# Two expert stages: 71 row tiles instead of 72, the first rows fetched at the end of the stage before, and another order for the first eight tiles

## The reference

```python
x = x + 0.5 * ffn(layernorm(x))        # expert stage 1
x = x + attention(layernorm(x))        # 16 heads of 8, causal
x = x + 0.5 * ffn(layernorm(x))        # expert stage 2
# ffn: each token belongs to one of 8 experts (the largest affinity), and is kept if its
# rank among the batch's tokens for that expert is under a capacity; a kept token gives
#   gelu(x @ W1[e] + b1[e]) @ W2[e] + b2[e]        (128 -> 512 -> 128)
# a token that is not kept goes through as zeros, which leaves a constant row of the biases
```

## Time and profile before

| | |
|---|---|
| timed runs (3) | 1042.62, 1045.26, 1045.6 us; median 1045.26 |
| profiled execution | 1035.15 us, its span 1033.3 us |
| PE busy | 896.4 us (87%) |
| DVE, ACT, POOL busy | 724.8, 607.5, 682.8 us |

### The profile page before, as it was taken

The page is one execution under the profiler, slowest core; times in us unless marked ns, Lnnn a source line. Parts: engine busy times, 40 slices in busy tenths (PEclk is TensorE's granted clock), DMA queues, the critical chain, the costliest instruction groups (busy, mean ns, idle before and its releaser), DMA issues. The chain is left out here.

```text
span 1033.3 us, 26499 instructions
## 1 busy us (share of the span) xinstructions
PE 896.4 (87%) x8219; PEld 679.6 (66%) x8219; DVE 724.8 (70%) x2368; ACT 607.5 (59%) x1581; POOL 682.8 (66%) x1247
## 2 busy tenths in 40 slices
PE   5937499999647999999999999999999873999995
PEld 5823399999623566565656666565656542999995
DVE  8879745444237889899998989998898845444441
ACT  2637366666313666676666666666666651766662
POOL 7709668643023678888888888888887773355554
PEclk9999799999958999999999999999999985999998
DMA  7450022223145544446354554545454102222220
GB/s 214 128 173 1 17 69 67 69 66 64 40 79 106 122 96 101 115 94 122 95 116 101 109 108 97 121 95 117 95 115 97 39 24 61 60 67 67 64 59 21
DMA packets 127407, 89.72 MB, mean 87 GB/s; under 512 B 14305, under 2 KB 117910, under 8 KB 127270
## 3 DMA queue, kind: packets, MB, share of 16 engines
q1 hardware_dynamic: 103078, 52.69, 22.8%
q10 hardware_dynamic: 15488, 17.74, 7.7%
q0 software_dynamic: 8704, 17.60, 6.6%
HBM read 52.23 MB, written 35.47 MB: 85 GB/s over the span
## 5 line engine op out<-in xcount | busy, mean ns | idle before, releaser
L1291 ACT ACTIVATE at_pt<-at_pm 128x512 f32<-128x512 f32 x384 | 228.5, 598 | 117.9 <-PE at_pm L1379 84.2
L1609 DVE TENSOR_REDUCE at_mx<-at_pp 128x2 f32<-128x512 f32 (+1 forms) x384 | 259.5, 678 | 44.7 <-PE at_pp L1368 37.1
L1207 POOL TENSOR_SCALAR_AFFINE_SELECT at_pt<-at_pt 128x256 f32<-128x256 f32 (+1 forms) x384 | 187.8, 493 | 57.4 <-ACT at_pt L1291 54.1
L925 ACT ACTIVATE e_ht<-e_ps_h,b1t 128x128 f32<-128x128 f32 x576 | 164.8, 370 | 98.2 <-PE e_ps_h L954 98.2
L964 PE MATMUL e_ps_y<-w,e_ht 128*128 x1152 | 159.2, 282 | 0.0
L954 PE MATMUL e_ps_h<-e_xnt,e_w1own 128*128 128x128 f32 x1152 | 154.8, 279 | 1.4 <-issue 1.4
L954 PEld LDWEIGHTS e_ps_h<-e_xnt,e_w1own 128*128 128x128 f32 x1152 | 143.0, 195 | 1.6 <-issue 1.6
L964 PEld LDWEIGHTS e_ps_y<-w,e_ht 128*128 128x128 f32 x1152 | 140.0, 192 | 1.7
L1011 DVE SCALAR_TENSOR_TENSOR e_y<-e_ps_y,e_x 128x256 f32<-128x256 f32 x72 | 30.6, 425 | 155.7 <-PE e_ps_y L964 155.7
L888 POOL DMA_INDIRECT out_dram<-e_y,e_x x72 | 73.6, 1022 | 86.4 <-DVE e_y L1011 74.8
L1400 PE MATMUL at_po<-at_pt,vp 128*32 128x256 f32 (+1 forms) x2048 | 109.8, 332 | 1.6 <-POOL at_pt L1207 1.6
(11 more groups left out here) (327 smaller groups left out, 1788.6 us busy)
## 6 DMA issues: line engine op xcount, KB each, us to landing
at_qkd<-at_part SPq DMA_DIRECT2D x64, 192.0 KB, 3.0
kb<-at_qkd SPq DMA_DIRECT2D x64, 96.0 KB
qs<-at_qkd ACTq DMA_DIRECT2D x64, 96.0 KB
e_x<-buckets SPq DMA_DIRECT2D x72, 66.0 KB, 1.9
x<-e_y SPq DMA_DIRECT2D x36, 128.0 KB, 1.8
rows<-ts_x ACTq DMA_DIRECT2D x16, 264.0 KB, 3.0
ts_x<-in_x_dram SPq DMA_DIRECT2D x16, 256.0 KB, 3.5
x_by_token<-at_xa SPq DMA_DIRECT2D x32, 128.0 KB
```

The costliest lines, as they stand in the source:

```text
L925: last = a.activation(hid_t[j % NB][:, f, :], ps_h[j % NB][:, f, :], ACT.Gelu, bias=c.b1t[:, ds(e, 1), f])
L1207: g.affine_select(out=tile, in_=tile, compare_op=ALU.is_ge, fill=0.0, base=0, pattern=[[0, n], [1, P]], channel_multiplier=-1).then_inc(ma ...
L1291: a.activation(pt[u % RING][:, :], pm[u % 2], ACT.Exp, scale=SCALE).then_inc(exped, 1)
L1609: v.tensor_reduce(out, src, axis=AX.X, op=ALU.max).then_inc(maxed, 1)
```

## The change

- `NTE = NT + E - 1 = 71` takes the place of `NS = 72` in `experts`: 36 pairs still, the last of one tile. The buffer `x1` in HBM is a tile shorter.
- `x_row` and its semaphores are made once, in `consts`, and live through all stages. So that they fit, `at_p` in `route` no longer has a buffer of its own but uses the buffers of `c.qs`, which attention fills later.
- At the end of `route`, POOL waits for `gidx` and issues the gathers of the first 16 tiles of e1. At the end of `attention`, SP waits for `base`, reads 16 row numbers, waits as before for the buckets, and issues the loads of the first 16 tiles of e2. DVE converts `base` before `eid` there. The stages themselves start with tile 16 (`HEAD_PAIRS = 8`).
- In `experts` the start is written out: on PE `turn_x(0)`, `expand(0)`, `expand(1)`, `turn_x(1)`, `contract(0)`, `expand(2)`, and so on, the register loads of the expert numbers come first on PE and after the first copy on ACT, and the wait for the constant rows and W2 stands before the first `contract`. On DVE two W1 copies stand before the first `keep`, the others between the normalisations.

The core of the diff:

```diff
+NTE = NT + E - 1
+NR, HEAD_PAIRS = 8, 8
@@ consts
+    c.x_row = [m.sb(f"e_x{k}", [P, 2, XW]) for k in range(NR)]
+    c.x_in = {tag: [m.sem(f"{tag}_xin{k}") for k in range(NR)] for tag in ("e1", "e2")}
@@ route
-        at_p = sb("atp", [P, NT, P], BF16)
+        at_p = [q[:, :, :].rearrange("p h s -> p (h s)").rearrange("p (n w) -> p n w", w=P) for q in c.qs]
@@ route, POOL
+            pool.wait_ge(gidx_done, 1)
+            for j in range(2 * HEAD_PAIRS):
+                pool.indirect_dma_start(c.x_row[j // 2][:, j % 2, :], None, io["rows"],
+                                        bass.IndirectOffsetOnAxis(ap=c.gidx[:, j:j + 1], axis=0)).then_inc(c.x_in["e1"][j // 2], 16)
@@ route, DVE
-            s.step(v.tensor_copy(c.gidx[:, 0:NS], gsrc[:, :]))
+            v.tensor_copy(c.gidx[:, 0:NS], gsrc[:, :]).then_inc(gidx_done, 1)
@@ experts
-        NU = NS // 2
+        NU = -(-NTE // 2)
@@ experts, POOL
-                for j in range(2 * NR):
-                    gather(j)
-                for j in range(NS - 2 * NR):
+                for j in range(NTE - 2 * HEAD_PAIRS):
@@ experts, SP
-                for j in range(NS):
+                for j in range(2 * HEAD_PAIRS, NTE):
@@ experts, ACT
+            turn_x(0)
+            e = experts_of(act, 0)
+            bend(0, e[0])
+            turn_x(1)
+            bend(1, e[1])
+            bend(2, e[2])
+            turn_x(2)
+            bend(3, e[3])
+            turn_x(3)
+            bend(4, e[4])
+            for i in range(1, NU):
@@ experts, PE, in contract
+                if j == 0:
+                    pe.wait_ge(c.cst_in, 16 * 3)
+                    pe.wait_ge(c.w2_in, 16)
@@ experts, PE
-            pe.wait_ge(c.cst_in, 16 * 3)
-            pe.wait_ge(c.w2_in, 16)
-            for i in range(-TURN, NU):
-                if i + TURN < NU:
+            e = experts_of(pe, 0)
+            turn_x(0)
+            expand(0)
+            expand(1)
+            turn_x(1)
+            contract(0, e[0])
+            expand(2)
+            turn_x(2)
+            contract(1, e[1])
+            expand(3)
+            turn_x(3)
+            expand(4)
+            for i in range(1, NU):
+                if TURN < i + TURN < NU and i > 2:
                     turn_x(i + TURN)
...
+                    if i <= 2 and j == 2 * i:
+                        turn_x(i + TURN)
@@ experts, DVE
-            for j in range(FETCH):
-                fetch(j, e[j])
-            for i in range(-NORM, NU):
+            fetch(0, e[0])
+            fetch(1, e[1])
+            for i in range(NORM):
+                keep(i)
+                norm(2 * i)
+                norm(2 * i + 1)
+                if i == 0:
+                    fetch(2, e[2])
+                    fetch(3, e[3])
+                if i == 2:
+                    fetch(4, e[4])
+            for i in range(NU):
+                if i == 0:
+                    fetch(5, e[5])
@@ attention, SP
-            sp.wait_ge(tailed, 16 * E)
-            for k in range(NQ):
-                sp.wait_ge(row_out[k], 32 * (B // NQ))
+            sp.wait_ge(based, 1)
+            for j in range(0, 2 * HEAD_PAIRS, 8):
+                _, r = nc.values_load_multi_w_load_instructions(
+                    c.base[0:1, j:j + 8], engines=[sp.engine], min_val=0, max_val=E * STRIDE,
...
+                if j == 0:
+                    sp.wait_ge(tailed, 16 * E)
+                    for k in range(NQ):
+                        sp.wait_ge(row_out[k], 32 * (B // NQ))
+                for i in range(j, j + 8):
+                    sp.dma_start(c.x_row[i // 2][:, i % 2, :], io["buckets"][ds(r[i - j], P), :]).then_inc(c.x_in["e2"][i // 2], 16)
```

More of the change, by code:

```diff
@@ L544, in route @@
         zeroed = sem("zeroed")
-        far_done, near_done = sem("far"), sem("near")
+        far_done, near_done, gidx_done = sem("far"), sem("near"), sem("gidx")
         NA = 2
@@ L599, in _ @@
                     act.wait_ge(iota_done, 1)
-                of = slice((g + 1) * TG - NA, (g + 1) * TG)
+                first = (g + 1) * TG - NA
+                of = at_p[first // PN][:, first % PN:first % PN + NA, :]
                 for n in range((g + 1) * TG - NA, (g + 1) * TG):
-                    last = a.activation(at_p[:, n, :], iotab[:, :], ACT.Abs, scale=-1.0, bias=colp[:, n:n + 1])
+                    last = a.activation(at_p[n // PN][:, n % PN, :], iotab[:, :], ACT.Abs, scale=-1.0, bias=colp[:, n:n + 1])
                 last.then_inc(far_done, 1)
                 act.wait_ge(far_done, g + 1)
-                a.activation(at_p[:, of, :], at_p[:, of, :], ACT.Relu, scale=-1.0, bias=1.0).then_inc(near_done, 1)
+                a.activation(of, of, ACT.Relu, scale=-1.0, bias=1.0).then_inc(near_done, 1)
                 act.wait_ge(s_done, g + 1)
@@ L643, in invert @@
                 for n in range(g * TG, (g + 1) * TG):
-                    last = te.matmul(ps_inv, at_p[:, n, :], at_t[:, :, n, :],
+                    last = te.matmul(ps_inv, at_p[n // PN][:, n % PN, :], at_t[:, :, n, :],
                                      start=(n == 0), stop=(n == NT - 1), skip_group_check=True)
@@ L805, in sem @@
             return t.sem(f"{tag}_{name}")
[L807 removed]
+        NU = -(-NTE // 2)
         OUTS = 16 if by_slot else 32
[L809 removed]
+        NN, NX, NB = 8, 3, 4
         NORM, TURN, FETCH, BEND = 4, 3, 4, 3
         IDS = 8
[L812 removed]
+        x_row, x_in = c.x_row, c.x_in[tag]
         y_row = [t.sb(f"{tag}_y{k}", [P, 2, D]) for k in range(NR)]
@@ L882, in _ @@
             else:
-                for j in range(NS):
+                for j in range(NTE):
                     s = (j // 2) % NR
@@ L909, in _ @@
             for k in range(NR):
-                sp.wait_ge(y_out[k], OUTS * len(range(k, NU, NR)))
+                sp.wait_ge(y_out[k], sum(16 if by_slot else 16 * tiles_of(i) for i in range(k, NU, NR)))
         @blk.scalar
@@ L944, in turn_x @@
                 wait(pe, x_tr_out, i - 1)
-                for j in (2 * i, 2 * i + 1):
+                for j in range(2 * i, upto(i)):
                     pe.wait_ge(xn_done, j + 1)
@@ L1185, in _ @@
             blank_tails(sp, 0)
-            sp.wait_ge(tailed, 16 * E)
-            for k in range(NQ):
-                sp.wait_ge(row_out[k], 32 * (B // NQ))
+            sp.wait_ge(based, 1)
+            for j in range(0, 2 * HEAD_PAIRS, 8):
+                _, r = nc.values_load_multi_w_load_instructions(
+                    c.base[0:1, j:j + 8], engines=[sp.engine], min_val=0, max_val=E * STRIDE,
+                    skip_runtime_bounds_check_because="a tile's first row is at most that of the blank rows behind the last bucket, E * STRIDE")
+                if j == 0:
[4 more added lines that the diff above has]
+                    sp.dma_start(c.x_row[i // 2][:, i % 2, :], io["buckets"][ds(r[i - j], P), :]).then_inc(c.x_in["e2"][i // 2], 16)
         @blk.gpsimd
```

67 lines of the change are left out of this document (36 added, 31 removed).

## The result

The changed kernel takes 1058.76 us (median of 4 runs, 1057.13 to 1059.99), the kernel before 1044.46 beside it: a ratio of 1.0137, 95% interval 1.0122 to 1.0153. That is +14.3 us, slower as forecast, and just over half of the +26.0 that was forecast.

A forecast was written before the change was run, and what follows sets the result against it. PE was taken to bound the running expert stages, with all engines meeting at stage ends. Terms of +18.3 us in e1 and +7.7 in e2 gave +26.0 on 1045.26: 1071 us forecast, range 1061 to 1077.

The forecast's parts named there:

- The moved gathers hold POOL and the meeting point: End of route: 16 gathers take 20.15 us beside nothing; with POOL's drain the meeting point moves +25.8 us.
- Rival C: Ends of route and attention: the issue doesn't hold the meeting points, only gains stand, -10.3 us, 1035; chance 0.06.
- Rival D: Route: gathers cost POOL only the instruction's 0.95 us each, 4.8 us less, +21, 1066; chance 0.06.
- I take 6.2: End of route: POOL's drain behind the moved gathers takes 6.2 us, as in e1; 3.3 was the lower end.
- rival A: End of route: the drain is short or overlaps, its six microseconds aren't paid, +19.8, 1065; chance 0.10.
- rival B: The drain grows with the burst to twice 6.2, or SP stalls again: +33.9, 1079; chance 0.06.
- e1's start, -5.5: From DVE's first e1 instruction, first finish at 12.2 us and third at 22.2 instead of 27.7: -5.5 us.
- 71 tiles: One tile less: -2.0 us of PE work in e1, -1.6 us in e2's tail of scatters on POOL.
- SP's loads, +10.5 less 1.2: 16 loads add 10.5 us at the end of attention; e2's start gets 1.2 us shorter.
- the long instruction: Among e2's loads on SP, one DMA instruction of 1.99 us instead of 0.33, counted in the 10.5 us.
- The term for 8.8: End of attention: SP's 16 loads cost 8.8 us if the one long DMA instruction is absent.
- The timed runs' median is 10.1 us above that execution and I add the same: Whole kernel: the profiled execution of 1035.15 us lies 10.1 us under the timed median; same offset added after the change.

The follow-up runs named there:

- after_again: The changed kernel run once more against the kernel before, on a chip of the 1034-us level: 1054.35 us, ratio 1.0190.
- before_third: The kernel before, unchanged, under a second name and traced, at the 1034-us level: ratio 1.0005 to the kernel before.
- after_third: The changed kernel run a third time against the kernel before, on a chip of the 1045-us level: 1059.80 us, ratio 1.0129.
- before_fourth: The kernel before, unchanged, under a second name and traced, at the 1045-us level: ratio 1.0006 to the kernel before.
- g0l0: The changed kernel with gathers and loads both back in their own stages, leaving 71 tiles and the new order: 1028.47 us, ratio 0.9934 to the kernel before.
- late_loads: The changed kernel with the 16 loads back in e2 and the gathers still in route: 1048.06 us, ratio 1.0133 to the kernel before.
- g0: The changed kernel with all 16 gathers back in e1 and the loads still in attention: 1036.01 us, ratio 1.0021 to the kernel before.
- the pause: The kernel before with 22 us of POOL memsets ahead of the end of route: 1055.84 us at the lower level, 1066.85 at the upper.
- old71: The kernel before with only the 71 tiles, nothing moved and the old order: 1042.31 us, ratio 0.9963 to the kernel before.
- g8: The changed kernel with 8 gathers in route, the other 8 in e1, loads kept in attention: 1052.97 us, ratio 1.0078 to the kernel before.

## Why the prediction was right in its direction and wrong in its size

The stages as the traces have them, in us: the forecast, the change at the 1034-us level (after_again less before_third) and at the 1045-us level (after_third less before_fourth, from two chips of that level).

| from ... to | forecast | 1034 | 1045 |
|---|---|---|---|
| start to S | +25.8 | +22.1 | +22.2 |
| S to third finish | -5.5 | -5.7 | -12.6 |
| third to last finish of e1 | -2.0 | -1.8 | -1.8 |
| last finish to `base` | 0 | -1.5 | +1.0 |
| `base` to third finish of e2 | +9.3 | +6.3 | +7.1 |
| from there to the end | -1.6 | -1.5 | +0.8 |
| sum | +26.0 | +17.9 | +16.7 |
| timed | | +20.3 | +14.4 |

(Single executions of the kernel before lie between 1029.5 and 1038.6 at the lower level, and its three traces there differ by up to 1.9 us in `attention` alone; the two chips of the upper level differ by 1.9 us in its median. So a column meets its timed difference only to about 3 us.)

- **The moved gathers hold POOL and the meeting point: right.** 20.0 us for 16 (forecast 20.15), with all other engines idle. Rival C is out. Rival D is out as well: the gaps of 0.30 us stayed. The Trainium skill says in "DMA: Bandwidth & Descriptors" (Issuing engines are not separate DMA queues) that the time to initiate a DMA is usually small relative to the DMA itself. The traces don't agree for these gathers: 1.25 us each on POOL, against 2.6 from issue to landing (median, before_third).
- **"I take 6.2" for the drain behind them: wrong.** It took 2.3; this is rival A's side, which I gave 0.10, and rival B, a drain that grows with the burst, is out. I had both ends, 3.3 and 6.2, and chose by likeness of the DMAs instead of by how many the stage had issued. 3.9 us too much, of which 0.7 came back since `gidx` was written that much later.
- **e1's start, -5.5: right in its working** (12.2 and 22.2 us against 12.0 and 22.0), from a trace without the stop. Only 2.6 us of it are the moved gathers' (g0l0 against after_again).
- **71 tiles: right in e1** (-1.8). In e2 -1.5 at the lower level. At the upper one the tail isn't to be read, since the pairs' pace differs between its two chips (4.11 and 4.07 us).
- **SP's loads, +10.5 less 1.2: too much.** 8.7 of busy time without the long instruction, 6.3 to 7.5 net by traces, late_loads and g0. The term for 8.8 was in the text, and I carried the long instruction over as if it were part of the loads. It isn't: all eight traces of the kernel before, with the pause or without, have one of 1.22 to 1.99 us among e2's first 16 loads, and no kernel of 71 tiles has one over 0.72, not even where the loads stay in e2 (old71: 0.54). So it belongs to the start of e2 in the kernel before; what makes it is not shown.
- **"The timed runs' median is 10.1 us above that execution and I add the same": the step that failed most.** The 10.1 us are not an offset that stands beside every kernel. before_fourth less before_third, 10.3 us of span, says where they are: 0.8 to S, 6.75 in e1's stop, 0.6 to the next pair, 1.3 in `attention`, and 1.9 in e2's pairs (4.07 against 4.01 us), less 0.4 before e2's first finish and 0.6 behind its last. The profiled execution of 1035.15 us has the lower level's first finish and e2 pair (139.12 and 4.01), the kernel after's the upper level's pair (4.11), and the timed runs of both the upper level's times. That the kernel before was profiled on one chip and timed on another is my reading of these; no row says it. The change removes its gathers from just where those 7 us lie. Worked over with what the later traces measured, the forecast is 26.0 - 3.9 + 0.7 - 3.0 (loads and e2's start, 9.3 against 6.3) - 6.9 (S to third finish, -12.6 against -5.7) = +12.9, beside +14.3 measured.

What would have shown it: a median 1% above the profiled execution, in a range of 3 us that doesn't reach down to it, was a sign that the trace and the times are of two conditions. And the timeline of the kernel before, with a first finish at 139.1, already held a small stop in front of the same tile, which I passed over:

```profile
136.95 1.13 PE L954 MATMUL e_ps_h<-e_xnt,e_w1own 128*128 128x128 f32 x8 [1.43 <-issue]
```

What makes the three engines wait in the stop is left open. The gathers beside it are necessary (after_third, g8), and so is something in which the chips differ. An instruction stream that comes late to PE's queue would look like PE's gaps, but it would not explain ACT and DVE, which wait for products that PE has already made by the trace. No row names it, nor semaphores that arrive late: queues 8 and 14, which carry instructions, moved no packet from 136 to 147 in before_fourth and one in before_third. Neither was tried.

## What to carry to other kernels

Work put ahead of a meeting point of all engines was paid here at its full issue time, and what it shortened behind it came back only in part: move a prefetch only where the issuing engine is idle longer than the issue takes. Size the cost of a stage's end from a stage that issued about as much, not by the nearest name, and keep all the ends that the trace shows in the range. Before adding a trace's terms to the timed median, see that the traced execution lies within the timed runs; if not, part of what the change touches may be missing from the trace. Of this change only the 71 tiles and the order (g0l0) are worth keeping where neither head moves: -4.9 to -5.6 us at the lower level; at the upper one 71 tiles with the old order give -2.1 to -3.1, and g0l0 wasn't run.

## What the runs showed of the hardware that was not expected

- Two levels of chips for one and the same program: medians of 1034.1 to 1035.9 us on two chips and 1043.6 to 1045.5 on two others.
- On the slower ones alone PE, ACT and DVE came nearly to a stop for 7 us beside POOL's gathers, and in three of its traces ACT and DVE started again within 0.04 us of each other; it moved by 21.2 us with the gathers and was gone without them. On the faster ones PE's gap at that place was 0.9 to 1.8 us.
- POOL's drain behind indirect DMAs: 1.7, 2.1, 2.3, 4.9 and 5.8 us after 2, 8, 16, 55 and 71 of them in the stage, but 3.3 after 128 in `attention`.
- 16 loads of 66 KB each held SP's queue for 8.7 us, 0.54 us apiece, where the DMA instruction itself took 0.33.
